# One block instead of two, expert weights loaded in the first stage, and sub-tile rows spread over all partitions

## What is computed

```python
xn = layernorm(x)
# attention at 12 sampled positions per head and token, within 8 tokens of it
q, k, v = xn @ wq.T + bq, xn @ wk.T + bk, xn @ wv.T + bv      # 16 heads of 16
off = tanh(pw(gelu(depthwise3(q)))) * 6
positions = clip(token + linspace(-2, 2, 12) + off, 0, Q - 1)
scores = q . sample(k, positions) / 4 - rel_scale * |positions - token|
s = (softmax(scores) . sample(v, positions)) @ wo.T + bo      # sample interpolates linearly
# top 2 of 8 experts
y = sum over 2 chosen e of gate_e * ((silu(xn @ W1a_e) * (xn @ W1b_e)) @ W2_e)   # with biases
out = x + s * silu(y)
```

## Time and profile before

| | |
|---|---|
| median of 3 runs | 1496.08 us (1493.31 to 1501.79) |
| profiled execution, span | 1494.3 us; the page gives no other time of it |
| TensorE matmul, busy | 1361.6 us (91%) |
| VectorE, busy | 1280.2 us (86%) |
| ScalarE, busy | 823.8 us (55%) |
| GpSimd, busy | 804.3 us (54%) |
| HBM traffic | 201 GB/s over the span |
| chain that ended last | VectorE 48%, DMA 8%, PE 8% of the span |

### The profile page before, as it was taken

How to read it: one execution, slowest core, us unless ns; L and a number is a source line. 1 busy time by engine, 2 the same in 40 slices (tenths; PEclk the granted TensorE clock), 3 DMA queues, 4 the chain that set the end, 5 groups by cost and what they waited for, 6 DMA issues and landing times.

```text
span 1494.3 us, 35841 instructions
## 1 busy us (share of the span) xinstructions
PE 1361.6 (91%) x13687; PEld 1085.4 (73%) x13688; DVE 1280.2 (86%) x1504; ACT 823.8 (55%) x1889; POOL 804.3 (54%) x566
## 2 busy tenths in 40 slices
PE   5998899984799999999999998999999978797988
PEld 4864565653688888888888886887888856675766
DVE  7837655556699999999999999999999999999961
ACT  2547687864445555555555554554555436574655
POOL 1001477773587766767666877768686651311111
PEclk9999999985999999999999999999999988898999
DMA  7933366564957676768677666767777679999897
GB/s 231 352 130 101 115 203 208 166 222 158 287 122 224 170 232 161 222 161 235 183 204 214 168 179 160 214 159 201 196 190 221 133 178 232 250 218 246 217 246 148
DMA packets 203481, 293.52 MB, mean 196 GB/s; under 512 B 24833, under 2 KB 160261, under 8 KB 203123
## 3 DMA queue, kind: packets, MB, share of 16 engines
q0 software_dynamic: 65792, 146.59, 38.5%
q1 hardware_dynamic: 134915, 144.84, 33.6%
q10 hardware_dynamic: 2672, 0.83, 0.2%
HBM read 182.83 MB, written 117.74 MB: 201 GB/s over the span
## 4 chain that ended last, share of the span: by engine, by line
DVE 48%; DMA 8%; PE 8%; issue 6%; SPq 5%; POOL 0%; ACT 0%; POOLq 0%; DVEq 0%
DVE gslope L1647 11%; DVE parts L1643 11%; DVE parts L1603 8%; DMA band<-band_rows 7%; DVE expert_mem L1569 5%; PE pB L1480 3%; DVE parts L1615 3%; SPq L1121 2%; DVE parts L1619 2%; DVE parts L1622 1%; PE pA L1465 1%; PE pY L1490 1%; DVE gslope L1700 1%; SPq L1115 1%; DVE wgt L1708 1%
## 5 line engine op out<-in xcount | busy, mean ns | idle before, releaser
L1175 POOL DMA_INDIRECT moe_rows<-expert_mem,token_of x142 | 324.9, 2288 | 76.2 <-issue 47.9
L1446 PE MATMUL pA<-xsT,expert_mem 128*128 128x256 f32 x1136 | 264.5, 387 | 22.6 <-DMA expert_mem<-in_w_l 15.5
L1156 POOL DMA_INDIRECT expert_mem<-xn_rows,token_of x142 | 222.3, 1566 | 96.8 <-issue 74.2
L1452 PE MATMUL pY<-expert_mem 128*128 x1136 | 265.7, 387 | 0.0
L1446 PEld LDWEIGHTS pA<-xsT,expert_mem 128*128 128x128 f32 x1136 | 220.3, 195 | 55.9 <-issue 20.0
L1446 PE MATMUL pB<-xsT,expert_mem 128*128 128x256 f32 x1136 | 256.8, 379 | 0.0
L1452 PEld LDWEIGHTS pY<-expert_mem 128*128 128x128 f32 x1136 | 211.1, 191 | 42.3 <-issue 16.2
L1446 PEld LDWEIGHTS pB<-xsT,expert_mem 128*128 128x128 f32 x1136 | 215.8, 190 | 29.3
L1643 DVE SCALAR_TENSOR_TENSOR parts<-pos_pair,prob 128x768 f32<-128x768 f32 x256 | 228.0, 953 | 1.1
L1647 DVE TENSOR_REDUCE gslope<-parts 128x256 f32<-128x3072 f32 x64 | 214.7, 3354 | 2.2
L1297 ACT ACTIVATE expert_mem<-pA,b1sel 128x256 f32<-128x256 f32 x284 | 111.3, 474 | 135.3 <-issue 93.2
(11 more groups left out here) (197 smaller groups left out, 2036.3 us busy)
## 6 DMA issues: line engine op xcount, KB each, us to landing
expert_mem<-in_w_l POOLq DMA_DIRECT2D x71, 1024.0 KB, 7.0
band<-band_rows SPq DMA_DIRECT2D x256, 96.0 KB, 5.5
S_rows<-stage SPq DMA_DIRECT2D x64, 376.0 KB
band_rows<-wgt SPq DMA_DIRECT2D x12, 1536.0 KB, 7.1
pos_pair<-pos_rows SPq DMA_DIRECT2D x28, 384.0 KB, 7.7
xn_rows<-stage SPq DMA_DIRECT2D x16, 512.0 KB, 5.4
v_rows<-stage SPq DMA_DIRECT2D x16, 512.0 KB, 4.2
moe_rows<-zeros POOLq DMA_DIRECT2D x4, 2048.0 KB
```

The source lines that it names most:

```text
L1156: nc.gpsimd.indirect_dma_start(out=xs[:, u, s], out_offset=None, in_=dram["xn"], in_offset=bass.IndirectOffsetOnAxis(ap=keep["inv"][:, 2 * ...
L1175: nc.gpsimd.indirect_dma_start(out=dram["moe"], out_offset=bass.IndirectOffsetOnAxis(ap=keep["inv"][:, 2 * n + s:2 * n + s + 1], axis=0), ...
L1446: mm = nc.tensor.matmul(dst[:, c], w1[:, 1 - u, k, o * HID + c * P:o * HID + (c + 1) * P], xsT[:, k], start=(k == 0), stop=(k == KC - 1))
L1452: mm = nc.tensor.matmul(pY[:, s], hid[:, h, c, s * P:(s + 1) * P], w2[:, c, ds(e * D, D)], start=False, stop=(s == 1 and c == HC - 1))
```

## The change

It has three parts.

**One block.** Both functions write into one block, so nothing but semaphores stands between them. W1, W2 and the gathered rows now lie in the memory of kT and of the front's staging tiles, and are loaded as soon as the front no longer needs that part. Engines that reuse the front's memory wait for its stores first (`front_over`).

**Early loads.** Two of the four W2 parts are loaded by SyncE with groups 8 and 9, the other two behind the last head scores; the first two W1 by GpSimd behind its third quarter of scatters; the first four row gathers at the end of GpSimd's front. The read of the slot list moves up on VectorE by three steps. `reload_slope(1)` moves ahead of wo, and ScalarE's `prepare(0)` behind the first evacuation and `take_expert`.

**Interleaved sub-tiles.** Sub-tile s of a tile no longer lies in partitions 32s to 32s+31 but in partitions s, s+4, s+8 and so on. Positions, slopes, weights and bands all follow, so `store_pos` becomes four DMAs, and TensorE reads `bandT` with a step of four numbers.

Core of the diff:

```diff
-BAND_SKEW = BAND - 1
+BAND_SKEW = SUBS * BAND - 1
+EARLY_FROM = GROUPS_PER_SEQ
+EARLY_W2 = SEQ // (EXPERTS * D)
...
-        stage = sb("stage", [P, 4 * GROUP_F])
+        stage = keep["shared"][:, STAGE_AT:STAGE_AT + 4 * GROUP_F]
...
-        block = ctx.enter_context(nc.Block())
+        block = keep["block"]
...
             def store_pos(n):
                 sp.wait_ge(pos_ready, n + 1)
-                sp.dma_start(dram["pos"][rows_of(n), :].rearrange("(a p) c -> p a c", p=P), pos[:, n % 2]).then_inc(
-                    pos_stored[n % 2], 16)
+                for s in range(SUBS):
+                    sp.dma_start(dram["pos"][rows_of(n), :].rearrange("(a t s) c -> s t a c", t=SUB, s=SUBS)[s],
+                                 pos[s * SUB:(s + 1) * SUB, n % 2]).then_inc(pos_stored[n % 2], 16)
...
                 if n == OPEN_AT:
                     load_opening()
+                if n >= EARLY_FROM and n < EARLY_FROM + EARLY_W2:
+                    sp.wait_ge(s_done, EARLY_FROM * GROUP)
+                    keep["load_w2"](sp, n - EARLY_FROM)
             store_pos(STEPS - 2)
+            sp.wait_ge(s_done, TILES)
+            for k in range(EARLY_W2, HC):
+                keep["load_w2"](sp, k)
             store_pos(STEPS - 1)
...
+            def first_w1():
+
+                pool.wait_ge(experts_known, 1)
+                pool.wait_ge(s_done, EARLY_FROM * GROUP)
+                for n in range(2):
+                    e = pool.value_load(keep["tile_exp"][0:1, n:n + 1], min_val=0, max_val=EXPERTS - 1)
+                    pool.dma_start(keep["w1"][:, 1 - n], io["w_l1"][ds(e, 1), :, :].rearrange("o (k p) n -> p (o k) n", p=P)).then_inc(
+                        keep["w1_loaded"][n], 16)
...
                 clear_moe(q)
+                if q == 2:
+                    first_w1()
...
             pool.wait_ge(gates_stored, 16 * 4)
+            pool.wait_ge(pads_set, 16 * 9)
+            for u in range(2):
+                pool.wait_ge(xn_stored[u], 16 * (STEPS // 2))
+            pool.wait_ge(tokens_known, 1)
+            for n in range(2):
+                for s in range(2):
+                    nc.gpsimd.indirect_dma_start(
+                        out=keep["xs"][:, n, s], out_offset=None, in_=dram["xn"],
+                        in_offset=bass.IndirectOffsetOnAxis(ap=keep["inv"][:, 2 * n + s:2 * n + s + 1], axis=0)).then_inc(
+                            keep["xs_loaded"][n], 16)
...
+            dve.wait_ge(list_loaded, 16)
+            chain(V.tensor_copy(list_f[:], spare_i[:]))
+            V.tensor_scalar(keep["inv"][:], list_f[:], float(TOKENS), None, ALU.add).then_inc(tokens_known, 1)
             offset_bias(STEPS - 1, 0)
             positions(STEPS - 2)
             offset_bias(STEPS - 1, 1)
-            dve.wait_ge(list_loaded, 16)
-            chain(V.tensor_copy(list_f[:], spare_i[:]))
-            V.tensor_scalar(keep["inv"][:], list_f[:], float(TOKENS), None, ALU.add)
             positions(STEPS - 1)
...
+        def front_over(eng):
+
+            eng.wait_ge(keep["front_pos_ready"], STEPS)
+            for stored, count in keep["front_stored"]:
+                eng.wait_ge(stored, count)
...
-            return bass.AP(dram["band"].tensor, (n * P + s * SUB) * BAND, [[BAND_SKEW, SUB], [1, BAND]])
+            return bass.AP(dram["band"].tensor, (n * P + s) * BAND, [[BAND_SKEW, SUB], [1, BAND]])
...
-                    sp.dma_start(band[s * SUB:(s + 1) * SUB, f], band_of(n, s)).then_inc(band_loaded[f], 16)
-
+                    sp.dma_start(band[s:P:SUBS, f], band_of(n, s)).then_inc(band_loaded[f], 16)
+
+            front_over(sp)
             sp.dma_start(b2[:], dram["bias"][:, :, 0:D]).then_inc(b_loaded, 16)
-            sp.wait_ge(w1_loaded[0], 16)
-            for k in range(HC):
-                sp.dma_start(w2[:, k].rearrange("p (e n) -> p e n", e=EXPERTS),
-                             io["w_l2"].rearrange("e (k p) n -> k p e n", p=P)[k]).then_inc(w2_loaded, 16)
+            reload_slope(1)
...
-            for it in range(1, 3):
-                reload_slope(it)
+            reload_slope(2)
...
-            for n in range(2):
-                load_xs(n, n)
-                load_w1(n, n)
+            front_over(pool)
...
-            prepare(0)
             evacuate_x(0)
             take_expert(0, 0)
+            prepare(0)
+            for stored in keep["front_sx_stored"]:
+                act.wait_ge(stored, 16 * STEPS)
...
-                                                  bandT[0:ROWS, u, q, s * SUB:(s + 1) * SUB], start=True, stop=True)
+                                                  bandT[0:ROWS, u, q, s:P:SUBS], start=True, stop=True)
...
+            pe.wait_ge(keep["front_s_ready"], TILES)
             transpose_x(0, 0, 0)
...
+            dve.wait_ge(keep["front_pads_set"], 16 * 9)
             V.memset(gslope[:, :, 0], 0.0)
...
-            return [(keep["slope"][q * SUB:(q + 1) * SUB].rearrange("p (a f jh) -> p f a jh", a=GROUP, f=2)[:, f],
+            return [(keep["slope"][q:P:SUBS].rearrange("p (a f jh) -> p f a jh", a=GROUP, f=2)[:, f],
...
+        def load_w2(eng, k):
+            eng.dma_start(keep["w2"][:, k].rearrange("p (e n) -> p e n", e=EXPERTS),
+                          io["w_l2"].rearrange("e (k p) n -> k p e n", p=P)[k]).then_inc(keep["w2_loaded"], 16)
```

More of the change, by code:

```diff
@@ L289, in front_block @@
         list_rows = sem("list_rows")
+        experts_known = sem("experts_known")
+        tokens_known = sem("tokens_known")
+        keep["front_pos_ready"], keep["front_s_ready"] = pos_ready, s_ready
+        keep["front_sx_stored"], keep["front_pads_set"] = sx_stored, pads_set
+        keep["front_stored"] = [(pos_stored[u], 16 * SUBS * (STEPS // 2)) for u in range(2)] + [(sx_stored[u], 16 * STEPS) for u in range(SX_SLOTS)]
+        keep["front_stored"] += [(pads_set, 16 * 9), (gates_stored, 16 * 4), (bias_stored, 16)]
         scattered = sem("scattered")
@@ L526, in bases @@
                 if n >= 2:
-                    act.wait_ge(pos_stored[n % 2], 16 * (n // 2))
+                    act.wait_ge(pos_stored[n % 2], 16 * SUBS * (n // 2))
                 for a in range(GROUP):
@@ L1002, in mix_block @@
         pJ = [pY[:, 0], pO[:, 0]]
-        w1_loaded = [sem(f"w1_loaded{u}") for u in range(2)]
-        w2_loaded = sem("w2_loaded")
+        w1_loaded, w2_loaded, xs_loaded = keep["w1_loaded"], keep["w2_loaded"], keep["xs_loaded"]
         wo_loaded = sem("wo_loaded")
@@ L1009, in mix_block @@
         b_loaded = sem("b_loaded")
-        xs_loaded = [sem(f"xs_loaded{u}") for u in range(2)]
         xsT_done = sem("xsT_done")
@@ L1773, in build @@
         keep["slopes_in"] = slopes_in
+        shared = keep["shared"] = sb("expert_mem", [P, SHARED_F])
+        keep["w2"] = shared[:, 0:W2_F].rearrange("p (k n) -> p k n", k=HC)
+        keep["w1"] = shared[:, W1_AT:W1_AT + W1_F].rearrange("p (u k n) -> p u k n", u=2, k=KC)
+        keep["xs"] = shared[:, XS_AT:XS_AT + XS_F].rearrange("p (u s c) -> p u s c", u=2, s=2)
+        assert TOKENS + 1 + 2 * REACH <= KT_PITCH and W1_F <= SEQ + 1 and XS_F <= 4 * GTOK * D // P - SX_SLOTS * (SUBS // 2) * S_ROW
+        for name in ("xs_loaded", "w1_loaded"):
+            keep[name] = [ctx.enter_context(nc.semaphore(f"{name}{u}")) for u in range(2)]
+        keep["w2_loaded"] = ctx.enter_context(nc.semaphore("w2_loaded"))
+        keep["sems"] = ctx
+        def load_w2(eng, k):
+            eng.dma_start(keep["w2"][:, k].rearrange("p (e n) -> p e n", e=EXPERTS),
+                          io["w_l2"].rearrange("e (k p) n -> k p e n", p=P)[k]).then_inc(keep["w2_loaded"], 16)
+        keep["load_w2"] = load_w2
+        keep["block"] = ctx.enter_context(nc.Block())
         with nc.sbuf_tensor("scores", [P, TILES, EXPERTS], F32) as scores, \
-                nc.sbuf_tensor("qT", [P, KC, BATCH * (SEQ + 2)], F32) as qT, \
-                nc.sbuf_tensor("kT", [P, KC, TOKENS + 1 + 2 * REACH], F32) as kT:
+                nc.sbuf_tensor("qT", [P, KC, BATCH * (SEQ + 2)], F32) as qT:
+            kT = shared[:, 0:KC * KT_PITCH].rearrange("p (c n) -> p c n", c=KC)
             keep.update(scores=scores, qT=qT, kT=kT)
```

49 lines of the change are left out of this document (23 added, 26 removed).

## The result

The changed kernel takes 1483.8 us at the median (1480.9 to 1491.3), the kernel before 1498.2 (1493.0 to 1504.5); the ratio is 0.9921, with a 95% interval from 0.9901 to 0.994. So it is faster by 12 us (9 to 15), where 22 were forecast. The profiled execution has a span of 1479.3 us, 15.0 under the 1494.3 of before; it is the fastest of the 13 executions of the changed kernel, so it shows more than 12.

A forecast was written before the change was run, and what follows sets the result against it. VectorE was taken to bound steps 0 to 11 and DMA time the end, with tiles and VectorE level before tile 42. Terms 14.0 + 2.6 + 7.0 - 1.5 = 22.1 us off 1496.1 gave 1474 us, range 1462 to 1487.

The forecast's parts named there:

- Start of step 0: Opening: products of step 0 start at 362.05 instead of 364.75 us, 2.7 us gained, between 4.0 and minus 0.8.
- Stalls of the opening: VectorE before products of step 1: all four stalls go, 11.3 us gained; the lower bound is half of that.
- Steps 0 to 11: VectorE's stretch after the opening: same instructions, no gain of its own, only moved by 14.0 us.
- End stage up to tile 42: Last steps: only VectorE's waits for ScalarE's gates go, 2.6 us gained, between 0 and 4.
- the signs: Profile if right: among others, ScalarE's exponentials at tiles 14, 28 and 42 wait for VectorE by several us each.
- After tile 42: Last 19 tiles: faster band transfers let them take 67.9 instead of 74.9 us, 7.0 us gained; ends 65.1 and no gain.
- Clock: TensorE at tile 42: the new wait brings a slower clock, costing 1.5 us, 0 to 3.
- The strided read: TensorE's 64 products per tile, operand read with a 16-byte step: costs nothing; other end 1.21 us a tile.
- my rival: TensorE's products: the strided read becomes the bound, 1.21 us a tile more, 1504 us in all; chance 0.08.
- Late next: End: weights of step 15, 10.5 us to store and 5.5 to load, leave tile 60 four us of slack.
- the forecast's own bounds: Whole kernel: 1464 to 1478 us around the forecast of 1474, given a chance of 0.53.
- The first rival: End stage: interleaving speeds up no DMA, gain only 14.0 + 2.6, 1479.5 us; chance 0.20 with a small strided-read penalty.

The follow-up runs named there:

- one_block_only: The changed kernel without its interleaving, one block and the early loads of step 0 kept: 1484.8 us, ratio 0.992 to the kernel before.
- interleave_only: The kernel before with the interleaving alone, two blocks as before: 1495.5 us, ratio 0.9977 to the kernel before.
- before_ahead: The kernel before with eight band slots instead of four and bands issued four tiles ahead: 1504.3 us, ratio 1.0053 to the kernel before.
- two_more_issues: The changed kernel with two more 4-byte loads a tile on SyncE, which nothing reads: 1502.8 us, ratio 1.0031 to the kernel before.
- plain_two_more: The changed kernel without its interleaving, with two more 4-byte loads a tile on SyncE: 1485.5 us, ratio 0.9913 to the kernel before.
- permuted_identity: The changed kernel with band columns put in order by the transposes, so products read neighbouring columns: 1483.5 us, ratio 0.9902 to the kernel before.
- one_load_ahead_45: The changed kernel with one band load a tile, eight slots from tile 8, last exponentials ahead of tiles 29 and 45: 1474.4 us, ratio 0.9834.

## Why the prediction was right or wrong

- **Start of step 0**, 2.7 us, bounds 4.0 to -0.8: 1.1. The chain of list, gathers and transposes came near its time (transposes at 359.11 us, 358 forecast); VectorE goes from `bends` into `products` without a wait. The list landed at 353.39 instead of about 349, which used up the 4 us in hand. But the front ends at 362.25 instead of 359.62, so VectorE's own end set the start; the prediction had named an end later than 360 as a sign of being wrong. Of these 2.6 us 2.0 were there ahead of the W1 loads, one execution against another, and 0.6 came behind them. W1's transfers, which I had only as GpSimd's issues, seem to cost some 2 us in other executions.
- **Stalls of the opening**, 11.3 us: 12.4 less 1.1, 11.3. Right, to the place where each stall stood, though with less in hand: SyncE issued the slopes by 379.5 us, where the forecast had slopes and positions out by 373.
- **Steps 0 to 11**: right, 738.9 against 739.2 us.
- **End stage up to tile 42**, 2.6 us: 14.75 less the 12.7 that the weights of step 11 were ahead, 2.0; VectorE's waits on this stretch fell from 5.0 to 3.0 us. That the interleaving did this is not shown: from the weights of step 11 to those of step 15 it is 234.1 us before, 232.0 after, but 233.7 in `one_block_only` and 234.2 in `interleave_only`. Of the signs only the exponentials at tile 42 waited by several us; those at 14 not at all, at 28 for 0.9.
- **After tile 42**, 7.0 us: nothing, and this is the step that failed. From two queues that "take 64.2% and 38.3% of the 16 engines' time" I concluded "So the end of the kernel is bound by DMA time", and counted the faster transfers as time. The speed came in full: the forecast's 10.87 MB in 41.0 us are 265 GB/s, measured are 267. But tiles 46 to 63 still take 4.0 us each, and the end comes 53.0 us behind the last weights (53.2 before). Between those tiles the waits for bands fell from 7.5 to 4.9 us only; the products, some 1.5 us longer by the strided read, and a mean granted clock of 0.93 instead of 0.95 stood against that. What the tiles waited for is not in my sum: a load is issued only when the tile four earlier is through, and with eight slots the same tiles take 3.5 to 3.6 us, at the old speed too (`before_ahead`). And the change took something in exchange, SyncE's room, as `two_more_issues` against `plain_two_more` shows: I priced the bytes of the four loads, and not their issues, which the change makes 30% longer (2.38 against 1.83 us); the row for an issue that I had (0.48 us) I used for the front alone. Whether DMA time would have bound the kernel before with all its tiles at TensorE's pace stays open. The term's lower end, "no gain", was right.
- **Clock**, -1.5 us: not to be told apart. Behind the wait at tile 42 the granted clock is 0.50 (1.2 GHz) from 1393 to 1398 us and four transposes take 1.09 us; from 1400 to 1412 it is 1.00 (2.4 GHz) and they take 0.64. But this lies among waits for bands that would have taken the time.
- **The strided read**, nothing: 0.09 us a tile, 5.8 us of TensorE over 64 tiles, hidden in waits (`permuted_identity`). The Trainium skill's "Memory Cachelines" (Advanced Engine Details and Errata) names a penalty where each access takes another line; the trace agrees in direction, at less than a tenth of the price that my rival gave it (0.09 against 1.21 us a tile).
- **Late next**: the weights of step 15 with 16 us to store and load. `one_load_ahead_45` shows this bound, at 16.5 us.

That 1483.8 us lies within the stated range, 1462 to 1487, is owed to the rivals that the range took in: the forecast's own bounds end at 1478. The first rival has nearly the measured time (1479.5), by a wrong reason: the interleaving does speed up the DMAs. By the Trainium skill's "What 'DMA-bound' means" (Perfetto Trace Analysis) a kernel can be bound on the issuing sequencer as well as on the engines; SyncE's rows of the changed kernel, solid at 3.55 us a tile in the stretch shown, agree, though over the whole end stage SyncE still waits for 25 us. I never weighed that case.

## What to carry to other kernels

Before a change of layout is credited with faster transfers, put four numbers of a tile side by side: the consumer's time, the transfers' time, the issuing queue's time with its gaps, and the delay from the freeing of a slot to the landing. The largest of the first three is the least that a tile can take; the delay counts against the time until the consumer comes to the same slot again, here four tiles. A queue that needs as long as the consumer has no room to make up a delay. A cheap test is to add tiny transfers: they load the queue and not the engines. And look for what stands fixed behind the stage: here everything behind the last weights.

## What was not expected of the hardware

- A load of 32 rows to every fourth partition takes SyncE 0.60 us to issue, to 32 neighbouring ones 0.46 (2.38 and 1.83 for four). In the slower loads the source rows lie four apart too, so which side makes the difference is open.
- One load of 128 rows with 32 as outermost count lands in 5.8 us at the page's median; with 4 as outermost count it moves under 100 GB/s and costs the kernel some 112 us.
- A moving operand read with a step of 16 bytes costs 7% (1.30 against 1.21 us for 64 products), not a multiple.
